# The output projection of attention in three fp32r products instead of one fp32 product, its right-hand side split by ScalarE and GpSimd

## Reference

```
q, k, v = split(x_norm @ w_qkv.T)                # 16 heads of 64 features, 2 sequences: 32 heads in all
dots = q @ k.T / 8
m = softmax(dots); diag = diagonal(m)             # a token is kept if its diagonal entry lies
keep = abs((diag - mean) / std) <= 1.5            # within 1.5 standard deviations
attn = softmax(where(keep_i and keep_j, dots, -1e30))
out = concat_heads(attn @ v) @ w_out.T + b_out    # the product that is changed
x = x + out
```

## Time and profile before

| | |
|---|---|
| time, median of 3 executions | 1895.53 us (1892.8 to 1896.35) |
| the profiled execution's own time | 1897.05 us |
| its span, first to last instruction | 1895.6 us |
| PE busy | 1777.5 us (94%) |
| DVE, ACT, POOL busy | 1326.0, 1148.9, 1172.7 us |
| granted TensorE clock, mean | 0.991 |

### The profile page before, as it was taken

The page is one execution under the profiler, slowest core; times in us unless marked ns, Lnnn a source line. Parts: engine busy times, 40 slices in busy tenths (PEclk is TensorE's granted clock), DMA queues, the critical chain, the costliest instruction groups (busy, mean ns, idle before and its releaser), DMA issues. The chain is left out here.

```text
span 1895.6 us, 29863 instructions
## 1 busy us (share of the span) xinstructions
PE 1777.5 (94%) x11043; PEld 1212.1 (64%) x11043; DVE 1326.0 (70%) x2493; ACT 1148.9 (61%) x1715; POOL 1172.7 (62%) x660
## 2 busy tenths in 40 slices
PE   8998999888999897899999999999999999999888
PEld 5883444334785663577777777777677777765466
DVE  5627899996345764767777777777677767778676
ACT  6326777853435447676767676766667676753554
POOL 5541777874453551377677776776767777777354
PEclk9999999999999999999999999999999999999999
DMA  2000000000001004122221222121212121200100
GB/s 100 1 1 1 1 0 1 1 0 1 0 1 50 1 1 101 36 60 56 52 60 47 61 49 66 43 67 47 60 36 71 47 60 47 57 24 12 50 6 17
DMA packets 43665, 66.03 MB, mean 35 GB/s; under 512 B 24769, under 2 KB 26177, under 8 KB 43265
## 3 DMA queue, kind: packets, MB, share of 16 engines
q1 hardware_dynamic: 43056, 63.54, 13.0%
q10 hardware_dynamic: 432, 0.59, 0.1%
q0 software_dynamic: 32, 0.00, 0.0%
HBM read 29.05 MB, written 1.24 MB: 16 GB/s over the span
## 5 line engine op out<-in xcount | busy, mean ns | idle before, releaser
L2422 POOL TENSOR_TENSOR at_e_lo<-at_e,at_e_hi 128x1024 fp32r<-128x1024 f32 x256 | 613.0, 2394 | 308.8 <-DVE at_e_hi L2397 301.8
L2179 ACT ACTIVATE at_e<-at_ps,at_dropped 128x1024 f32<-128x1024 f32 x256 | 285.7, 1116 | 216.2 <-PE at_ps L1892 200.4
L2276 DVE CUSTOM_DVE_ANT_0 at_ps<-at_ps,at_mask 128x1024 f32<-128x1024 f32 x256 | 313.4, 1224 | 5.9 <-PE at_ps L2012 5.9
L2171 ACT ACTIVATE at_ps<-at_ps,at_neg_diag 128x1024 f32<-128x1024 f32 x256 | 278.5, 1088 | 42.2 <-DVE at_neg_diag L2267 41.9
L2397 DVE CAST at_e_hi<-at_e 128x1024 fp32r<-128x1024 f32 x256 | 228.5, 892 | 23.5 <-ACT at_e L2179 20.0
L1971 PE MATMUL at_ps<-at_kq,at_qk 64*128 64x512 f32 x768 | 222.0, 397 | 13.0 <-DMA at_kq<-at_qk 5.2
L2021 PE MATMUL at_ps<-at_qk,at_kq 64*128 64x512 f32 x768 | 225.1, 399 | 1.6 <-DVE at_row_max L2276 1.1
L1892 PE MATMUL at_pv_ps<-at_e_hi,at_v_hi 64*128 64x512 f32 x980 | 225.7, 453 | 0.3 <-issue 0.3
L2022 PE MATMUL at_ps<-at_kq,at_qk 64*128 64x512 f32 x768 | 225.0, 399 | 0.0
L1972 PE MATMUL at_ps<-at_qk,at_kq 64*128 64x512 f32 x768 | 222.2, 397 | 0.0
L1056 POOL TENSOR_TENSOR mb_work<-mb_work,mb_c 128x1024 f32<-128x1024 f32 x64 | 151.8, 2372 | 96.8 <-DVE mb_work L1025 96.7
(11 more groups left out here) (392 smaller groups left out, 4149.9 us busy)
## 6 DMA issues: line engine op xcount, KB each, us to landing
at_kq<-at_qk SPq DMA_DIRECT2D x128, 256.0 KB, 4.3
at_mask<-at_mask_dram SPq DMA_DIRECT2D x32, 256.0 KB, 3.6
at_recips<-at_recip_row SPq DMA_DIRECT2D x31, 256.0 KB, 4.4
ffn_h_raw<-in_h SPq DMA_DIRECT2D x2, 1024.0 KB, 7.3
at_head_w_raw<-in_w_qkv SPq DMA_DIRECT2D x32, 64.0 KB, 3.9
x<-in_x SPq DMA_DIRECT2D x4, 256.0 KB, 4.8
moe_gate_in<-in_gate_in SPq DMA_DIRECT2D x2, 512.0 KB, 3.9
moe_up_in<-in_up_in SPq DMA_DIRECT2D x2, 512.0 KB, 4.5
```

What stands on the lines that cost most here:

```text
L2171: act.eng.activation(ps[:], ps[:], ACT.Exp, scale=SCALE, bias=m.small["neg_diag"][s][:, blk:blk + 1], accum_out=m.small["sums"][s][:, blk: ...
L2179: act.eng.activation(m.e[e % 2][:], slot("turned_scores", h, blk)[:], ACT.Exp, scale=SCALE, bias=m.small["dropped"][h % SLOTS][:, blk:blk ...
L2276: dve.eng.tensor_tensor_reduce(out=ps[:], in0=ps[:], in1=m.mask[h % 2][:], scale=1.0, scalar=-BIG, op0=ALU.add, op1=ALU.max, accum_out=m.s ...
L2422: pool.eng.tensor_tensor(m.e_lo[e % 3][:], m.e[e % 2][:], m.e_hi[e % 3][:].bitcast(F32), ALU.subtract).then_inc(sem["at_lo"])
```

## The change

The product of `w_out` and `heads_out` is made of three fp32r products for all pairs but the last. For this ACT rounds `w_out` once and POOL makes its rest (at the start of attention). Per head 0 to 29, ACT rounds the normalized half of `heads_out` at the end of the step after the normalization (offset 38, step 6), and POOL makes the rest behind the `e_lo` of the third step after it (offset 40, step 0). The counter `at_norm` now counts two events per head (normalization and rest), which `normed(h)` translates; a POOL write to `heads_out` waits for the rounding two heads before instead of for the projection. Buffers per head (`SLOTS`: queries, keys, statistics) go from five to four.

```diff
-SLOTS = 5
+SLOTS = 4
+PAIRED = NH - 2
+def normed(h):
+    return min(2 * h + 1, 2 * PAIRED + 1)
@@ attention_later_norm_act, attention_later_norm_pool
+    act.eng.activation(m.w_out_parts[0][:], m.w_out[:], ACT.Copy).then_inc(sem["at_wv_hi"])
+    pool.wait_ge(sem["at_wv_hi"], 2)
+    pool.eng.tensor_tensor(w_lo[:], m.w_out[:], w_hi[:].bitcast(F32), ALU.subtract).then_inc(sem["at_wv_lo"])
@@ project_out
-            pe.wait_ge(sem["at_norm"], h + 1)
+            pe.wait_ge(sem["at_wv_lo"], 2)
+            pe.wait_ge(sem["at_norm"], normed(h) + 1)
             slot_free(pe, c, m, "out", h)
-        mm = both_rows([ps[:, half] for half in HALF], m.w_out[:, pair, :], [m.heads_out[:, half] for half in HALF],
-                       not turned, turned, turned)
+        (w_hi, w_lo), (hi, lo) = m.w_out_parts, m.heads_parts
+        for n, (w, x) in enumerate(((w_hi, hi), (w_lo, hi), (w_hi, lo))):
+            mm = both_rows([ps[:, half] for half in HALF], w[:, pair, :], [x[:, half] for half in HALF],
+                           n == 0 and not turned, n == 2 and turned, turned)
@@ attention_pe
-                if apart:
+                if h != LAST:
                     project_out(h, turned)
@@ attention_act
+    def round_heads(h):
+        place = slice(HD, P) if h % 2 else slice(0, HD)
+        act.wait_ge(sem["at_norm"], normed(h))
+        if h >= 2:
+            act.wait_ge(sem["at_out"], h // 2)
+        act.eng.activation(m.heads_parts[0][place, :], m.heads_out[place, :], ACT.Copy).then_inc(sem["at_heads_hi"])
...
+        if (at := due(t, AT_NORM + 1)) and at[0] < PAIRED:
+            round_heads(at[0])
@@ attention_pool
-                pool.wait_ge(sem["at_out"], h // 2)
+                pool.wait_ge(sem["at_heads_hi"], h - 1)
...
+        if (at := due(t, AT_NORM + 3)) and at[0] < PAIRED:
+            h = at[0]
+            pool.wait_ge(sem["at_heads_hi"], h + 1)
...
+            pool.eng.tensor_tensor(lo[place, :], m.heads_out[place, :], hi[place, :].bitcast(F32),
+                                   ALU.subtract).then_inc(sem["at_norm"])
```

More of the change, by code:

```diff
@@ L68 @@
     "moe_w_hi", "moe_xn_hi", "moe_scores", "moe_silu", "moe_comb_hi", "moe_hi",
-    "at_wv_hi", "at_xn_hi", "at_qk_hi", "at_v_hi", "at_sum", "at_dev", "at_exp", "at_pv_out",
+    "at_wv_hi", "at_xn_hi", "at_qk_hi", "at_v_hi", "at_sum", "at_dev", "at_exp", "at_pv_out", "at_heads_hi",
 )
@@ L1790, in attention_later_norm_pool @@
     pool.eng.tensor_tensor(m.wv_lo[:], m.wv_raw[:], m.wv_hi[:].bitcast(F32), ALU.subtract).then_inc(sem["at_wv_lo"])
-    pool.wait_ge(sem["at_wv_lo"], 1)
+    pool.wait_ge(sem["at_wv_hi"], 2)
+    w_hi, w_lo = m.w_out_parts
+    pool.eng.tensor_tensor(w_lo[:], m.w_out[:], w_hi[:].bitcast(F32), ALU.subtract).then_inc(sem["at_wv_lo"])
+    pool.wait_ge(sem["at_wv_lo"], 2)
 def load_head_weights(c, m, h):
@@ L2077, in project_out @@
         else:
-            pe.wait_ge(sem["attn_out_load"], 16)
-            pe.wait_ge(sem["at_norm"], h + 1)
+            pe.wait_ge(sem["at_wv_lo"], 2)
+            pe.wait_ge(sem["at_norm"], normed(h) + 1)
             slot_free(pe, c, m, "out", h)
-        mm = both_rows([ps[:, half] for half in HALF], m.w_out[:, pair, :], [m.heads_out[:, half] for half in HALF],
-                       not turned, turned, turned)
+        (w_hi, w_lo), (hi, lo) = m.w_out_parts, m.heads_parts
+        for n, (w, x) in enumerate(((w_hi, hi), (w_lo, hi), (w_hi, lo))):
+            mm = both_rows([ps[:, half] for half in HALF], w[:, pair, :], [x[:, half] for half in HALF],
+                           n == 0 and not turned, n == 2 and turned, turned)
         if turned:
@@ L2091, in project_out_alone @@
         pe.wait_ge(sem["attn_out_load"], 16)
-        pe.wait_ge(sem["at_norm"], min(h + 1, LAST))
+        pe.wait_ge(sem["at_norm"], normed(LAST - 1))
         slot_free(pe, c, m, "out", h)
@@ L2215, in attention_act @@
             if h:
-                act.wait_ge(sem["at_norm"], h)
+                act.wait_ge(sem["at_norm"], normed(h - 1))
             if h < LAST:
@@ L2335, in last_norm @@
             dve.wait_ge(sem["at_pv_out"], LAST + 2 * hf + 2)
-            dve.wait_ge(sem["at_norm"], LAST)
+            dve.wait_ge(sem["at_norm"], normed(LAST - 1))
             dve.eng.tensor_tensor(step, m.pv_ps[HD:, HALF[hf]], inv, ALU.mult).then_inc(done)
@@ L2405, in norms_before @@
     def norms_before(t):
-        return min(max(t - AT_NORM + BLK - 1, 0) // BLK, LAST)
+        normed = min(max(t - AT_NORM + BLK - 1, 0) // BLK, LAST)
+        return normed + min(max(t - AT_NORM - 3 + BLK - 1, 0) // BLK, PAIRED)
     for t in range(AT_FIRST, AT_LAST):
@@ L2430, in attention_pool @@
             if h:
-                pool.wait_ge(sem["at_norm"], h)
+                pool.wait_ge(sem["at_norm"], min(2 * h, 2 * PAIRED + 1))
             if h >= 2:
-                pool.wait_ge(sem["at_out"], h // 2)
+                pool.wait_ge(sem["at_heads_hi"], h - 1)
             pool.eng.tensor_tensor(m.heads_out[place, :], m.pv_sb[0:HD, :], m.recips[:],
                                    ALU.mult).then_inc(sem["at_norm"])
+        if (at := due(t, AT_NORM + 3)) and at[0] < PAIRED:
+            h = at[0]
+            place = slice(HD, P) if h % 2 else slice(0, HD)
+            hi, lo = m.heads_parts
+            pool.wait_ge(sem["at_heads_hi"], h + 1)
+            pool.wait_ge(sem["at_lo"], min(t - AT_TURNED + 1, NH * BLK))
+            pool.wait_ge(sem["at_w_lo"], min((t - AT_SPLIT) // BLK + 1, NH))
+            pool.eng.tensor_tensor(lo[place, :], m.heads_out[place, :], hi[place, :].bitcast(F32),
+                                   ALU.subtract).then_inc(sem["at_norm"])
     pool.wait_ge(sem["x_attn"], ATTN_SUMS)
@@ L2449, in attention @@
         m.w_out = sb("at_w_out", [P, HEADS // 2, P])
+        m.w_out_parts = [sb(f"at_w_out_{part}", [P, HEADS // 2, P], F32R) for part in ("hi", "lo")]
         m.xn_hi = sb("at_xn_hi", [P, TOK], F32R)
@@ L2483, in attention @@
         m.heads_out = sb("at_heads_out", [P, SEQ])
+        m.heads_parts = [sb(f"at_heads_{part}", [P, SEQ], F32R) for part in ("hi", "lo")]
         m.small = {k: [sb(f"at_{k}{i}", [P, BLK]) for i in range(SLOTS)] for k in
```

## The result

| | before | after |
|---|---|---|
| time, median | 1894.76 us (4 executions, 1892.8 to 1896.35) | 1953.62 us (4 executions, 1950.63 to 1961.78) |
| the profiled execution's own time | 1897.05 us | 1961.78 us |
| its span | 1895.6 us | 1960.5 us |
| PE busy | 1777.5 us | 1798.3 us |
| granted TensorE clock, mean | 0.991 | 0.979 |

The change makes the kernel slower: the ratio is 1.0304 [1.0286, 1.0322]. The forecast was 1943 us with 1915 to 1966 around it; direction and range hold, and the median lies 10.6 us above the number.

A forecast was written before the change was run, and what follows sets the result against it. PE was taken to bound the heads' steady part, POOL the end of attention. Waits of 44.9 us plus 6.4 at the end minus 3.9 gain gave +47.4 us, so 1943 us, range 1915 to 1966.

The forecast's parts named there:

- steady waits, 20 heads: Steps 2 and 3 of heads without a values projection in step 2: PE waits 1.74 us per head for DVE's maxima.
- steady waits, 7 heads with values: Heads 2, 6, ... 26: the values projection in step 2 covers the second wait, leaving 1.44 us per head.
- end of attention: Rests of heads 27 to 29 meet POOL's full queue: 1.41 us plus 2 x 2.52 us, together 6.4 us.
- TensorE's gain: Output projection as six fp32r pairs instead of fp32: 0.30 us less each, 13 times up to head 25, 3.9 us.
- the prediction's own signs of being wrong: `keep` and step 1's copy not stretched, `turn_mask` finding maxima ready, or POOL idle between rest and `e_lo` beyond DVE's 0.63 us.
- Who goes first: Whether POOL's rest or DVE's copy starts first at 1097.64, in step 1: called a matter of 0.05 us.
- main line: Rest before DVE's copy: copy kept back, PE waits 1.44 us in step 2, 1.74 in all; 44.9 us over heads 0-26.
- the alternative: Copy before rest: wait in step 2 goes, step 3's is about 0.2 us longer; some 44 us instead of 44.9.
- ACT's copy: Rival: ACT's rounding makes `e` of step 7 0.3 us late per head, reaching PE: +56 us, 1952 us; chance 0.10.
- The lag: Rival: DVE's maxima of step 2 are in time, only the end pays: +2.5 us, 1898 us; chance 0.09.
- Faster: Rival: POOL's rests lie in idle time everywhere, PE's gain remains: -4.5 us, 1891 us; chance 0.07.

The follow-up runs named there:

- (1): Changed kernel with POOL's rest per head replaced by a one-column memset, the low part staying zero: 1895.56 us, ratio 0.9988 to the kernel before.
- (12): Changed kernel with POOL's rest made for only 512 of the 1024 columns of each head: 1911.28 us, ratio 1.0069 to the kernel before.
- (4): Changed kernel with rounding and rest once per two heads, all 128 rows, for odd heads at offset 40: 1929.29 us, ratio 1.0162.
- (2): Changed kernel with rounding and rest still made but the projection as the old single fp32 product: 1962.19 us, ratio 1.0342.
- experiment 6: Changed kernel with one rest per pair of heads at offset 42 and the output projection at offset 44: 1915.49 us, ratio 1.0087.
- experiment 3: Changed kernel with POOL's rest one step earlier, at offset 39 (step 7), same instructions: 1940.32 us, ratio 1.0229.
- experiment 7: Changed kernel with one rest per pair of heads at offset 43 and the output projection at offset 45: 1907.56 us, ratio 1.0050.
- (11): Changed kernel with one rest per pair of heads, made by DVE behind its maxima of step 7 instead of by POOL: 1908.09 us, ratio 1.0049.

## Why the prediction was right, and where it was off

**Direction and mechanism: right, and shown.** POOL's rest delays its `e_lo`, that holds `keep`, `keep` holds the copy and the maxima of step 2, and PE, which already stood at those maxima, waits in `turn_mask`. Taking the rest away takes the loss away (1); half of its length leaves a wait of 0.65 us (12); half as many rests give half the loss (4); the product has no part in it (2).

| term | predicted | profile after |
|---|---|---|
| steady waits, 20 heads | 20 x 1.74 = 34.8 us | 20 x 1.79 = 35.8 us |
| steady waits, 7 heads with values | 7 x 1.44 = 10.1 us | 5.0 us |
| end of attention (measured: with what follows) | 6.4 us | 5.5 us |
| TensorE's gain | -3.9 us | -5.7 us |
| half clock in twelve heads | none | 17.7 us |
| other steps, and ahead of the heads | none | 3.9 + 2.5 us |
| sum | 47.4 us | 64.7 us |

Of the prediction's own signs of being wrong one came true: the copy of step 1 was not stretched (0.69 us). Also, the rests last 2.87 us on the average instead of 2.39, and PE waits at L1996 alone, not at L1989. All three come from the order of copy and rest, the next point.

**Who goes first: wrong in the main line, right in the alternative.** The step "the rest runs from 1097.69 to 1100.08, DVE's copy is kept back" did not occur in the head shown: the copy came first, the rest was held, step 2 had no wait and all of it came in step 3. That is what the prediction had worked out from the Trainium skill's rule (SBUF — State Buffer, SBUF: two separate sides), that whoever starts first keeps the ports; the trace agrees, in both directions (the rest 2.89 us behind a copy; the copy 2.85 us behind an `e_lo` in experiment 6). For the heads with values it mattered: 0.71 us instead of 1.44 (the alternative said 0.9), 5 us in total. The alternative's sum for all heads, 44 us, stands against 40.8 measured. In the other heads the sum of both waits is the same within 0.05 us.

**TensorE's gain: right kind, size off.** 0.30 us was the difference between the whole step pair with a projection and six pairs at 0.23 us. The measured pair of steps is 0.44 us shorter in step 4 and about 0.04 longer in step 3. So the projection in its new form costs 1.66 - 0.40 = 1.26 us instead of 1.36.

**The end of attention: near in size, in part by luck.** The prediction had POOL's full queue there and nothing else. In the trace PE waits in step 3 of heads 27 and 28 (1.28 and 1.89 us, then 2.81 us between its starts), and a stretch at half clock follows each time: steps 3 and 4 together take 3.0 and 3.3 us more. Steps 5 and 6 of the second are 2.5 us shorter, the last steps add 2.1 us, and what follows attention is 0.3 us shorter. So 5.5 us doesn't confirm the term: part of it is the clock, which the term had not counted.

**The term that was missing: the clock.** The prediction took PE's speed as constant, and this is the step that failed in size. A wait in PE was priced at its own length; twelve of the twenty long ones cost 1.5 us more. That the waits are the cause is shown by 2, 3 and 12 together: the product doesn't matter, the same POOL work with shorter waits has none, a wait of 0.65 us has none. In the changed kernel the starts of PE's matmuls around a long wait are 2.15 to 2.34 us apart; in experiment 3, where the largest around `mean` and `square` is 1.93 us, none was followed by a half clock. Why eight of the twenty were not followed by one, no run here tells.

The other three executions of the changed kernel took 1950.63, 1952.5 and 1954.73 us. The first two have a higher mean clock (0.985, 0.983), so they probably had fewer such stretches; they have no trace, so this is argued, not shown. The third has 0.979, as the profiled one, and is 7 us shorter all the same, which stays unexplained. Against their median the prediction's sum lacks 10.6 us, less than the 17.7 us of the profiled one. That the time lies inside the range is luck as far as the clock goes: the range reached up to 1966 because idle time might be missing, not because a stretch at half clock was thought of.

**Rivals.** ACT's copy doesn't show at the size of its rival, 9 us (1). The lag was not swallowed. "Faster" was the right account of what remains when the rest is free (1, -2 us), and no kernel tried with the rest made in full reached it. The best of them, experiment 7 and the rest on DVE (11), are still slower than before by 0.5%.

## What to carry to other kernels

Before work is put on GpSimd, look at what VectorE does beside it: even an instruction on 8 columns waited until a 2.4 us GpSimd instruction was over, and with in-order queues the delay goes to everything behind it. A late instruction has to be followed one step further than its own, to what it now runs beside. And a wait on TensorE costs more than its length when the clock falls after it: two kernels with the same work and nearly the same number of waits (the changed one and experiment 3) differ by 13 us (ratios 1.0304 and 1.0229), and the faster one has no such stretch in the heads. When GpSimd's time doesn't depend on the rows, as here (2.85 us with 128 rows, 2.87 with 64), use all 128.

## What the runs showed of the hardware

- The granted clock fell to 0.50 for 3.4 us after 12 of 20 gaps of 2.15 to 2.34 us between PE's starts, and after none of those up to 1.93 us in experiment 3. It did so after 9 of 20 such gaps in experiment 2 and 4 of 13 in experiment 4, and there once after gaps of 1.27 and 1.88 us, one behind the other. Each stretch in the changed kernel cost about 1.5 us.
- DVE's fp32 subtraction of 128x1024 elements with both operands in SBUF was held until POOL's instruction was over and ended 1.08 us behind it (14 of 15; the one that began 0.16 us before POOL's took 1.21 us); a cast ended 0.55 us behind the earlier trace rows, `keep` on 8 columns 0.03 us behind (1122.33 to 1122.36).
- POOL can be held as well: its rest of 2.39 us took 2.89 us when a DVE copy had begun 0.06 us earlier and ended 0.63 us after the rest's start.
